# Two mixtures of experts in a small transformer: the fronts run one group further ahead, the routing is spread over other steps, and the second layer becomes four 64x64 tiles

## What is computed

```
# layer 0, after h = h + attention(layernorm(h)):   6 experts, two hidden layers
rh = relu(x @ router_w1 + router_b1)
logits = softmax(rh @ router_w2 + router_b2);  top_w, top_i = top_k(logits, 2)
weights = softmax(top_w)
h1 = relu(x @ expert_w1 + expert_b1)           # every expert, every token
h2 = relu(h1 @ expert_w2 + expert_b2)
out = h2 @ expert_w3 + expert_b3;  h = h + sum over the two chosen experts of weight * out

# layer 1:   8 experts, one hidden layer
probs = softmax(x @ router_w.T);  top 2, their weights divided by their sum
out = x + sum over the two chosen of weight * (gelu(x @ w1 + b1) @ w2 + b2);  h = h + out
```

## Time and profile before

| | before |
|---|---|
| median of three runs | 763.96 us |
| the profiled execution | 764.58 us, of which the trace spans 762.8 us |
| PE busy | 645.8 us (85%) |
| DVE busy | 516.0 us (68%) |
| ACT busy | 312.6 us (41%) |
| POOL busy | 188.6 us (25%) |
| mixture 0 | 216 to 435 us of the span |
| mixture 1 | 568 to 763 us of the span |

### The profile page before, as it was taken

One profiled execution on the slowest core, in us unless ns is written; L12 is line 12 of the kernel. 1 busy time (PEld: TensorE's weight loads), 2 busy tenths in 40 slices (PEclk: granted clock), 3 DMA queues, 4 the chain that ended last, 5 costly groups with the idle time before them and its releaser, 6 DMA issues. The chain is left out here.

```text
span 762.8 us, 16178 instructions
## 1 busy us (share of the span) xinstructions
PE 645.8 (85%) x6175; PEld 416.5 (55%) x6175; DVE 516.0 (68%) x1531; ACT 312.6 (41%) x707; POOL 188.6 (25%) x202
## 2 busy tenths in 40 slices
PE   2899999799966999999998898998765888888884
PEld 2875655599943445454443476887663444334432
DVE  3767797476833666566756469999754767777773
ACT  0100111155423665555563445776542353344442
POOL 1000002455441104121002075886513112121000
PEclk9999999899976999999997999999855779999998
DMA  9998950000000000000000000000000000000001
GB/s 301 410 344 307 288 211 2 1 1 2 2 1 0 1 1 2 1 1 1 1 1 0 1 1 1 1 2 1 2 1 1 6 14 19 17 17 17 18 21 27
DMA packets 28125, 38.98 MB, mean 51 GB/s; under 512 B 19344, under 2 KB 19600, under 8 KB 28048
## 3 DMA queue, kind: packets, MB, share of 16 engines
q1 hardware_dynamic: 19232, 35.46, 13.1%
q10 hardware_dynamic: 8816, 2.49, 1.8%
HBM read 35.25 MB, written 2.69 MB: 50 GB/s over the span
## 5 line engine op out<-in xcount | busy, mean ns | idle before, releaser
L419 POOL TENSOR_TENSOR centred<-h,mean 82x512 f32<-82x512 f32 x64 | 66.7, 1042 | 427.5 <-DVE rstd L408 256.1
L1549 DVE TENSOR_TENSOR m_hm<-bank,m_h 128x656 f32<-128x656 f32 x112 | 93.6, 836 | 81.4 <-PE bank L1339 65.8
L1221 ACT ACTIVATE m_h<-bank,m_b 128x656 f32<-128x656 f32 x112 | 90.3, 806 | 109.1 <-PE bank L1323 73.9
L280 PE MATMUL bank<-cols,tok_weight 64*64 64x328 f32 (+1 forms) x1800 | 114.0, 409 | 17.7 <-DVE cols L318 15.8
L280 PEld LDWEIGHTS bank<-cols,tok_weight 64*64 64x64 f32 x1800 | 75.7, 135 | 52.9 <-issue 18.0
L317 DVE COPY cols<-image 128x1992 f32<-128x1992 f32 x32 | 62.1, 1949 | 17.5 <-DMA image<-in_x_dram 15.8
L421 POOL TENSOR_TENSOR xn<-centred,rstd 82x512 f32<-82x512 f32 x64 | 66.7, 1043 | 5.0
L1347 PE MATMUL bank<-m_h,m_w 128*128 128x328 f32 x192 | 66.7, 471 | 0.0
L1323 PE MATMUL bank<-m_xt,m_w 64*64 64x328 f32 x512 | 55.2, 504 | 6.4 <-ACT m_h L1221 5.0
L1359 PE MATMUL bank<-m_hm,m_wo 64*64 64x328 f32 x512 | 51.4, 470 | 6.4 <-DVE m_osb L1556 6.0
L1227 ACT ACTIVATE m_h<-bank,m_b 128x656 f32<-128x656 f32 x48 | 38.7, 807 | 37.1 <-PE bank L1347 36.9
(11 more groups left out here) (177 smaller groups left out, 1183.7 us busy)
## 6 DMA issues: line engine op xcount, KB each, us to landing
image<-in_x_dram SPq DMA_DIRECT2D x32, 1000.0 KB, 11.2
out_dram<-m_fin SPq DMA_DIRECT2D x16, 164.0 KB
tok_weight<-in_L_tok_weight_dram ACTq DMA_DIRECT2D x2, 400.0 KB, 8.5
m_w<-in_L_ffn_w_dram ACTq DMA_DIRECT2D x2, 128.0 KB
m_sel_raw<-c_sel_dram ACTq DMA_DIRECT2D x1, 256.0 KB
m_w<-in_L_ffn_expert_w_dram ACTq DMA_DIRECT2D x2, 96.0 KB
m_sel_raw<-c_sel_dram ACTq DMA_DIRECT2D x1, 192.0 KB
m_bo_raw<-in_L_ffn_expert_b_dram ACTq DMA_DIRECT2D x9, 1.5 KB
```

Source lines behind the costliest of these rows:

```text
L280: return pe.matmul(sum_bank[u % 2][s][t * D:(t + 1) * D, L * j0:L * j1], weight[s * R:(s + 1) * R, c, :], cols[u % 2][s * R:(s + 1) * R, c ...
L419: pool.tensor_tensor(self.centred[:], slots(self.h, g), mean.broadcast_to([L, G, D]), ALU.subtract).then_inc(self.shifted, 1)
L1221: act.activation(h1[n % RING][:], h1_bank, ACT.Gelu if last else ACT.Relu, bias=W.b1[:, k:k + 1]).then_inc(h1_ready, 1)
L1549: dve.tensor_tensor(hm[k][:], cb_bank, src[n % RING][:], ALU.mult).then_inc(hm_ready, 1)
```

## The change

It touches only the mixtures and what they load.

1. `FRONT` goes from 3 to 4: four fronts are made ahead of the first group, and the front of group g + 4 is made in group g, so the last four groups have none. POOL still makes three groups ahead of the stage (`AHEAD`). The second half of the layer norm's statistics is inverted one group earlier in mixture 0 (`delay` is gone).
2. The routing of a pair is spread over other steps (`ROUTE`), and is finished at step 1 of the group before the pair starts, not at its last step.
3. On PE, in mixture 0, `turn` stands behind `layer2`, `router` at the end of step 0, and `logits` directly ahead of `turn_output`. In mixture 1 `logits` stands ahead of `sum_pair`.
4. In mixture 0 `layer1`, `spread` and `layer2` are issued as 64x64 tiles. The second layer has no zeros any more: expert e of half s goes from rows 64e to columns 64((e + s) mod 2), so in half 1 the two experts have changed places. The biases `b2`, the weights `wo` and the selection `c_sel0` are loaded in both arrangements, and `hidden2` becomes two activations of 328 columns, one for each half.

```
-        ROUTE = {(0, 2): (0,), (0, 3): (1,), (1, 0): (2,), (1, 1): (3,), (1, 2): (4,), (1, 3): (5, 6, 7)}
-        COMBINE, SECOND = 3, (1, 0)
+        ROUTE = {(0, 0): (1, 2), (0, 1): (3,), (0, 2): (4,), (1, 0): (5, 6), (1, 1): (7,), (1, 3): (0,)}
+        COMBINE, SECOND = 3, (0, 1)
...
-        ROUTE = {(0, 2): (0,), (1, 0): (1, 2), (1, 1): (3, 4, 5), (1, 2): (6, 7)}
-        COMBINE, SECOND = 2, (1, 0)
+        ROUTE = {(0, 0): (0, 1), (0, 1): (2,), (0, 2): (3, 4), (1, 0): (5, 6), (1, 1): (7,)}
+        COMBINE, SECOND = 2, (0, 1)
...
+    def pair_of(g, r):
+        return g // 2 + 2 if last and r == 0 else (g + 2) // 2 if g % 2 == 0 else (g + 1) // 2
...
-                    act.activation(h2[n % RING][:], h2_bank, ACT.Relu, bias=W.b2[:, k:k + 1]).then_inc(h2_ready, 1)
+                    for s in (0, 1):
+                        ins = act.activation(h2[n % RING][:, s, :], h2_bank[:, s, :], ACT.Relu, bias=W.b2[:, s, k:k + 1])
+                    ins.then_inc(h2_ready, 1)
...
                     for s in (0, 1):
-                        mm = pe.matmul(h2_bank[:, s, :], W.w2[:, k, :], h1[n % RING][:, s, :], start=True, stop=True)
+                        for e in (0, 1):
+                            rows, at = slice(e * D, (e + 1) * D), (e + s) % 2
+                            mm = pe.matmul(h2_bank[at * D:(at + 1) * D, s, :], W.w2[rows, k, :], h1[n % RING][rows, s, :], start=True, stop=True)
...
-                            mm = pe.matmul(o_bank[cols, 0:HALF], W.wo[:, k, :], hm[k][:, s, :], start=(k == 0), stop=False)
+                            mm = pe.matmul(o_bank[cols, 0:HALF], W.wo[:, s, k, :], hm[k][:, s, :], start=(k == 0), stop=False)
...
-                for f in range(FRONT):
-                    take_logits(f)
-                    if f == 1:
-                        for k in range(2):
-                            route(0, k)
-                for k in range(2, 8):
+                take_logits(0)
+                take_logits(1)
+                for k in range(2):
                     route(0, k)
+                take_logits(2)
+                for k in range(2, 4):
+                    route(0, k)
+                take_logits(3)
+                for k in range(4, 8):
+                    route(0, k)
+                if last:
+                    route(1, 0)
```

More of the change, by code:

```diff
@@ L164, in build @@
         xn = [[sb(f"xn{i}{p}", [L, G * D]) for p in range(3)] for i in (0, 1)]
-        norm = [LayerNorm(sem, f"ln{i}", shared, xn[i % 2], i == 1) for i in range(4)]
+        norm = [LayerNorm(sem, f"ln{i}", shared, xn[i % 2]) for i in range(4)]
         stage_patches(nc, A, banks, h, stats, ident, ident16, attn, moe, norm[0])
@@ L431, in after_dve @@
             mine.vary(dve, 1)
-        if mine is not None and g == 2 + mine.delay:
+        if mine is not None and g == 2:
             mine.invert(dve, 1)
@@ L442, in after_act @@
     def after_act(act, g, mine, following):
-        if mine is not None and g == 1 + mine.delay:
+        if mine is not None and g == 1:
             mine.root(act, 1)
@@ L1006, in moe_weights @@
     if not last:
[L1007 to L1008 removed]
+        W.w2 = sb(tag + "w2", [128, NP, D])
+        W.b2 = sb(tag + "b2", [128, 2, NP])
         W.br1 = sb(tag + "br1", [2 * RH, 1])
@@ L1031, in load @@
                 get(W.b1[s * D:(s + 1) * D, :], b_in.rearrange("(k e) h -> e h k", e=2)[s])
-                get(W.wo[s * D:(s + 1) * D, :, :], w_out.rearrange("(k e) h d -> e h k d", e=2)[s])
+                for i in range(S):
+                    get(W.wo[s * D:(s + 1) * D, i, :, :], w_out.rearrange("(k e) h d -> e h k d", e=2)[(s + i) % 2])
             for r in range(3):
@@ L1047, in load @@
                     get(W.wr2[2 * RH:2 * RH + 1, s * EP:s * EP + E], A["L0_ffn_router_b2"].rearrange("(a e) -> a e", a=1))
-            if not last:
-                for e in range(E):
-                    s = e % 2
-                    get(W.w2[s * D:(s + 1) * D, e // 2, s * D:(s + 1) * D], A["L0_ffn_expert_w2"][e])
     def prepare(dve):
@@ L1238, in _ @@
                         router_hidden(f)
+                    if f == 1 and not last:
+                        exponents(0)
+                    if f == 2:
+                        weight_of_second(0)
                 if last:
                     copy_x(FRONT)
-                else:
-                    exponents(0)
-                weight_of_second(0)
                 combine(0)
+                if not last:
+                    exponents(1)
                 hidden1(0, 0)
@@ L1320, in layer1 @@
                         rows = slice(s * D, (s + 1) * D)
-                        if last:
-                            for e in (0, 1):
-                                mm = pe.matmul(h1_bank[e * D:(e + 1) * D, s, :], W.w1[rows, 2 * k + e, :], xt[g % len(xt)][rows, :], start=True, stop=True)
-                        else:
-                            mm = pe.matmul(h1_bank[:, s, :], W.w1[rows, 2 * k:2 * k + 2, :], xt[g % len(xt)][rows, :], start=True, stop=True)
+                        for e in (0, 1):
+                            mm = pe.matmul(h1_bank[e * D:(e + 1) * D, s, :], W.w1[rows, 2 * k + e, :], xt[g % len(xt)][rows, :], start=True, stop=True)
                     mm.then_inc(h1_done, 1)
@@ L1333, in spread @@
                         rows = slice(s * D, (s + 1) * D)
[L1334 to L1339 removed]
+                        for e in (0, 1):
+                            mm = pe.matmul(cb_bank[e * D:(e + 1) * D, s, :], W.sel[rows, 128 * k + D * e:128 * k + D * e + D], ct[g % 2][rows, s:G:2, :],
+                                           start=True, stop=True)
                     mm.then_inc(cb_done, 1)
@@ L1413, in step0 @@
                         before(g, k, spread)
+                        layer2(g, k)
                         if k == 0 and exists(f):
                             turn(f)
-                        if k == 1 and exists(f):
-                            logits(f)
-                        layer2(g, k)
-                        if k == 0 and exists(f):
-                            router(f)
-                        if k == 1 and exists(g - 1):
-                            turn_output(g - 1)
+                        if k == 1:
+                            if exists(f):
+                                logits(f)
+                            if exists(g - 1):
+                                turn_output(g - 1)
                         if k == COMBINE and exists(g + 1):
@@ L1427, in step0 @@
                             finish_sum(g - 1)
+                        if k == 0 and exists(f):
+                            router(f)
                 def step1(g):
@@ L1436, in step1 @@
                         spread(g, k)
+                        if k == 1 and exists(f):
+                            logits(f)
                         before(g, k, sum_pair)
@@ L1439, in step1 @@
                             finish_sum(g - 1)
-                        if k == 1:
-                            if exists(f):
-                                logits(f)
-                            if exists(g - 1):
-                                turn_output(g - 1)
+                        if k == 1 and exists(g - 1):
+                            turn_output(g - 1)
                         if k == COMBINE:
```

69 lines of the change are left out of this document (31 added, 38 removed).

## The result

The changed kernel takes 754.5 us (median; 753.3 to 755.7), the kernel before 763.8 in runs beside it (763.1 to 769.3). The ratio is 0.986, with a 95% interval from 0.982 to 0.991: 1.4% less time, where 3.0% was forecast. The direction is right, and the interval leaves out 1; the size is less than half of the forecast. 754.5 lies outside the forecast's own range (734 to 749) and inside the wide one (732 to 756), which takes in a rival, the meeting of DVE and POOL. The profiled execution has a span of 752.9 us, 9.9 less than before.

A forecast was written before the change was run, and what follows sets the result against it. PE was taken to bound mixture 0 (92% busy), PE and DVE waiting for each other mixture 1. Terms of -13.3 (mixture 0) and -9.6 (mixture 1) took 764.6 to 741.7, forecast as 741 us; own range 734 to 749, wide 732 to 756.

The forecast's parts named there:

- the meeting of DVE and POOL: Rival, mixture 1: POOL also holds up routing parts 5 and 6 in odd groups, so mixture 1 gains nothing; 750 us, 14%.
- Tiles side by side: Mixture 0, `layer2`: as eight 64x64 tile instructions it takes 0.78 us instead of 1.35, 0.57 us less a step.
- the first rival: Mixture 0, `layer2`: tiles writing one bank are put one after the other, so it stays at 1.35; 759 us, 10%.
- A pair of mixture 0: Two groups of mixture 0 save 1.4 us; six pairs that still make a front give -8.4 us.
- Prologue: Fourth front ahead of the first group delays mixture 0's first transposes (L1311) by 3.7 us; the same order costs mixture 1 0.8.
- At group 2 the layer norm's 1.75 us and two parts of the routing meet: +1: Mixture 0, group 2: DVE has both ahead of the first `weigh`, costing 1 us once.
- With the clock kept, group 13 gains 4.1: Mixture 0: fewer routing parts meet POOL, PE waits 1.3 us, -4 in the sum; 0 if the clock falls.
- A pair of mixture 1, -1.8: Gains 3.3 us from waits and `logits`, loses about 1.5 to routing ahead of `weigh`; 4.5 pairs give -8.1 us.
- The start of mixture 1: Rival: the slow stretch from 585 to 625 us changes by luck of order, giving 734 or 748 us; 9%.
- Groups without fronts: Mixture 0, groups 13 to 15: no front in either kernel, so they keep the full 2 x 0.57 us; -3.4 us.
- PE's clock: Rival: PE's clock falls in mixture 0 as new waits leave it some 80% busy; 806 us, slower, 5%.
- below 0.95 between 250 and 400 us: Sign of being wrong: PE's granted clock under 0.95 in this stretch of the changed kernel.

## Why the prediction was right or wrong, step by step

The forecast gain was 22.9 us and the profiled spans show 9.9. Mixture 0 gave 5.0 of 13.3: the missing 8.3 are 4.4 at groups 2 and 3, 2.8 from group 11 on, 0.8 in the steady groups and 0.4 in the prologue. Mixture 1 gave 5.3 of 9.6: 7.7 are missing behind group 3, and 3.4 came unforecast at its start.

- **Tiles side by side: right.** `layer2` takes 0.73 us (0.78 forecast). The rule of the Trainium skill (TensorEngine Tiling (Array Packing), Restrictions and Gotchas) that row tiles cannot use one bank at the same time, which was the first rival, has no cost here: eight instructions that write one bank from both halves of the rows, in different partitions, in 0.73 us.
- **A pair of mixture 0: right.** 1.2 us instead of 1.4, with the new wait of 0.63 (0.7 forecast) and without the one for `cp`. What I did not see is how much of the tiles' worth the new order took: 1.0 us a pair, by the run with the order of before.
- **Prologue: right.** +4.1 us, +3.7 forecast. Of the 4.1, 0.8 lay ahead of mixture 0's first `turn` (217.0 for 216.2). Between the third logits and the first `turn_combine` stand 7.5 us, where the forecast had 7.6. Mixture 1's +0.8 does not show in its first row, which is 1.5 us shorter.
- **"At group 2 the layer norm's 1.75 us and two parts of the routing meet: +1": mis-sized.** The period was 3.8 us longer than a steady one, and the run with the later root gives 3.4 of them back. I counted DVE's instructions and left ACT out. The change also moved ACT's square root from behind group 2 to behind group 1, right behind the instructions that make its input; I should have named what is queued behind it (hidden1, then the copy of x, then `router`). Another 1.7 us in group 3, from POOL's normalisations in a row (three; the first two fall beside parts 5 and 6), is not in the sum at all; with POOL gated there the period was 2.4 us shorter.
- **"With the clock kept, group 13 gains 4.1": wrong.** The group gained 0.8 us beyond what a group without a front gains: its period stood 6.8 us above the one behind it before, and stands 6.0 above it now. The wait is 2.90 us, not 1.3, and the clock fell behind it, for which the forecast had a gain of 0. I counted a hold-up for single two-operand instructions, and the casts between them were held up too. The run with POOL moved behind them gives the 5.5 us, so the place and the cause were right and the size of the wait was not.
- **A pair of mixture 1, -1.8: the step that cost most.** "Each of POOL's two instructions holds one of them up for 0.5 or so" was said of the even group alone. It is 0.8 each in the odd group, which had none in the sum (1.08 and 1.15 for 0.29 and 0.36), and 0.4 and 0.8 in the even one; up to 650 us PE also fell to half clock behind the wait. Instead of -8.1 over the nine places behind group 3 it gave -0.4: +5.0 in the first five and -5.4 in the last four. Once POOL is through a pair gains 2.8, most of the 3.3 that stood on the gain side; POOL takes 2.7 of it, where I had 1.5. This is the rival "DVE and POOL meet more often", to which I gave 14% and 750 us. The sign named for this step came as well: `weigh` in the odd group starts 2.8 us into step 0 (644.73; `layer1` at 641.96), and 1.5 was the limit. The rival said that it needs casts that POOL holds up; the Trainium skill has that (SBUF — State Buffer, Who interferes with whom: copies and casts within SBUF can run in a mode that takes the port pair shared with GpSimd), and the rows of after agree, 1.15 us for 0.36. I had looked only for a row, and the trace of before has none with such a cast beside POOL; that sentence would have made the rival likelier.
- **The start of mixture 1: luck.** Forecast was +0.3 us, and it gave -3.1 (20.5 and 26.3 us became 19.0 and 24.8), with a granted clock of 0.84 from 585 to 625 where it was 0.67. No run takes this apart, and without it the time would have been about 758, outside the wide range.
- **Groups without fronts: right** (9.1 us for 10.1 and 11.1), but the last one gained nothing.
- **PE's clock: in between.** It did not fall in the steady groups of mixture 0, as forecast, but it fell behind two of the three single waits, and in mixture 1 behind four waits of 1.25 to 3.1 us up to 650 us (not behind those of 1.25 to 1.57 after that); the granted clock there is 0.92. I had named "below 0.95 between 250 and 400 us" as a sign of being wrong; apart from group 2 that stretch was at full clock. The sign did not come, though groups 2 and 3, both in that stretch, took 5.5 us more than two steady ones.

## What to carry to other kernels

When an instruction is moved, look at what else runs at its new place on the engines that share a resource with it: here the routing was moved to the very steps in which POOL normalises, and a gate of one line on POOL, which had time to spare, gave 9.0 us in its first form, about as much as the whole change (9.3); with the gate two groups later and one square root moved it was 19.4. A step that has a chain behind it over two engines (variance on DVE, root on ACT, inverse on DVE, then POOL) wants a group of distance between its links, and whoever shortens it should ask for every link what is queued behind it. Parts of a change need not add up: in mixture 0 tiles alone and order alone gave -5.2 and +5.3 us, both -9.1, and the tiles with four fronts and the routing, but PE's order of before, 8 us more than the whole change.

## What the runs showed of the hardware

- A cast from f32 to bf16 within SBUF that starts while POOL's instruction runs ends only behind it, as a two-operand instruction does (1.15 us for 0.36, 1.14 for 0.30); one that starts 0.3 us ahead of POOL's keeps its 0.36. `weigh` and `output`, which read one operand from PSUM, keep 0.82 and 0.50 us beside POOL.
- One square root in ACT costs two table loads of 1.28 us in mixture 1, one for the root and one for the next hidden layer; in mixture 0 the hidden layers run on with the root's table, and the second load comes with the next exponential.
- PE's waits of 1.83, 2.44, 2.90 and (mixture 1) 1.25 us were each followed by instructions at half clock (1.37 for 0.78, 1.30 for 0.73). Waits of 1.00 and 1.07 us in mixture 0 were not, nor was the one of 2.36 us in group 3, nor, in mixture 1 of the changed kernel, those of 1.57, 1.25 and 1.53 us between 657 and 678 us. So the length of a wait alone did not tell what it would cost, and I can't say from these runs what does.
